# Tile 1's norm moved ahead of the first flag, with the checks of weights spread among the opening's work

## What is computed

```
xn  = layernorm(x)
out = x + attn(xn) + ffn(xn)
attn: x1 = xn + dwconv3(xn);  n = ln(x1)
      act = silu(n @ actp_w + b);  xi = silu(dwconv3(n @ in_w + b))
      q, k = elu(xi @ qk_w + b) + 1;  linear attention with rope over 16 heads, + dwconv3(v)
      x1 += (attention * act) @ out_w;  x1 += dwconv3(x1);  x1 += gelu(ln(x1) @ fc1) @ fc2
ffn:  h = silu(xn w1) * (xn w2);  h = gelu(h h1);  h = gelu(h h2);  out = h w3      (ternary weights)
```

## Time and profile before

| | us |
|---|---|
| median of 3 runs | 1124.96 |
| lowest, highest | 1118.63, 1132.96 |
| the profiled execution's own time | 1125.7 |
| its span in the trace | 1123.7 |
| mean granted clock of TensorE | 0.977 |

### The profile page before, as it was taken

The page is one execution under the profiler, slowest core; times in us unless marked ns, Lnnn a source line. Parts: engine busy times, 40 slices in busy tenths (PEclk is TensorE's granted clock), DMA queues, the critical chain, the costliest instruction groups (busy, mean ns, idle before and its releaser), DMA issues.

```text
span 1123.7 us, 17165 instructions
## 1 busy us (share of the span) xinstructions
PE 1044.5 (93%) x6636; PEld 922.7 (82%) x6636; DVE 767.7 (68%) x950; ACT 592.8 (53%) x853; POOL 282.2 (25%) x232
## 2 busy tenths in 40 slices
PE   3779988999999999899998999999989999999997
PEld 3557876888777677678877889899889899999997
DVE  6685567554546647988787538669677787776764
ACT  3356766666624345455544545465545456555543
POOL 3243334331514241442333003203300111011100
PEclk9899989999999999899999999999999999999999
DMA  8859963544585455212440084252486331332310
GB/s 333 323 188 310 346 206 113 187 160 161 172 328 197 136 183 206 93 55 97 169 150 38 37 327 160 77 169 76 134 301 260 113 110 50 104 113 76 113 38 20
DMA packets 68337, 180.67 MB, mean 161 GB/s; under 512 B 4976, under 2 KB 26096, under 8 KB 64624
## 3 DMA queue, kind: packets, MB, share of 16 engines
q1 hardware_dynamic: 68256, 179.56, 46.0%
HBM read 121.86 MB, written 66.06 MB: 167 GB/s over the span
## 4 chain that ended last, share of the span: by engine, by line
PE 68%; DVE 13%; ACT 6%; DMA 5%; issue 5%; POOL 2%; SPq 1%; DVEq 0%; ACTq 0%; POOLq 0%
PE pr L2078 42%; PE pr L192 12%; PE pr L2245 7%; DVE x L1465 3%; DVE h_lo L1702 2%; PE pr L178 2%; PE pr L185 2%; PE pr L2056 1%; DMA xn_s<-xh 1%; DMA qa<-q_s 1%; DVE acc L1495 1%; PE pr L2200 1%; DVE full L1567 1%; DMA h_s<-silu 1%; ACT h_hi L1280 1%
## 5 line engine op out<-in xcount | busy, mean ns | idle before, releaser
L2078 PE MATMUL pr<-xp_hi,wb 128*128 128x256 f32 x1344 | 323.1, 283 | 6.9 <-DVE u L1830 4.0
L2078 PE MATMUL pr<-xp_lo,wb 128*128 128x256 f32 x1344 | 322.5, 283 | 0.0
L2078 PEld LDWEIGHTS pr<-xp_hi,wb 128*128 128x128 f32 x1344 | 257.4, 192 | 9.0 <-issue 9.0
L2078 PEld LDWEIGHTS pr<-xp_lo,wb 128*128 128x128 f32 x1344 | 258.0, 192 | 0.0
L2078 PE MATMUL pr<-u_hi,ring 128*128 128x512 f32 x256 | 102.3, 399 | 2.3 <-issue 1.3
L2078 PE MATMUL pr<-u_lo,ring 128*128 128x512 f32 x256 | 100.0, 391 | 0.0
L1024 POOL TENSOR_TENSOR ot<-ot,yg 128x512 f32<-128x512 f32 x14 | 25.2, 1805 | 253.2 <-DVE ot L1861 253.2
L1340 ACT CAST xp_hi<-tf 128x1024 fp32r<-128x1024 f32 x48 | 50.2, 1047 | 65.1 <-PE pr L2078 24.2
L1702 DVE TENSOR_TENSOR h_lo<-hf,h_hi 128x512 fp32r<-128x512 f32 x64 | 59.8, 953 | 23.8 <-ACT h_hi L1280 23.8
L2245 PE MATMUL pr<-wf_hi,h_hi 128*128 128x256 f32 x256 | 75.0, 293 | 0.0
L1824 DVE TENSOR_TENSOR xp_lo<-tf,xp_hi 128x1024 fp32r<-128x1024 f32 x48 | 60.8, 1266 | 19.9 <-ACT xp_hi L1340 19.8
(11 more groups left out here) (224 smaller groups left out, 2583.2 us busy)
## 6 DMA issues: line engine op xcount, KB each, us to landing
ring<-w_s SPq DMA_DIRECT2D x42, 512.0 KB, 5.2
uf<-h_s SPq DMA_DIRECT2D x16, 1024.0 KB, 5.8
wb<-s_s SPq DMA_DIRECT2D x8, 1024.0 KB, 8.7
stage<-w_gated SPq DMA_DIRECT2D x4, 1536.0 KB, 10.4
wb<-w_s SPq DMA_DIRECT2D x6, 1024.0 KB, 10.0
vw<-v_s SPq DMA_DIRECT2D x8, 514.0 KB, 6.6
xt<-x SPq DMA_DIRECT2D x8, 512.0 KB, 6.5
xn_s<-xh SPq DMA_DIRECT2D x8, 512.0 KB, 8.1
```

The costliest lines, as they stand in the source:

```text
L2078: return e.matmul(bank, w.bitcast(dt), v_.bitcast(dt), start=first, stop=last, skip_group_check=True)
```

## The change

Everything concerns the opening and step -1.

- SyncE issues `save_xn(0)` after the second `stage` load and the load of tile 3, ahead of the third and fourth `stage` loads.
- Tile 1's `conv1_side`, `norm_tokens`, `norm_moments`, `inverse_deviation`, `norm_offsets`, `apply_norm`, `norm_back`, `high_of_norm` move from step -1 into the opening, before the first flag. `low_of_norm(1)` on VectorE comes right after the flag. In step -1 these are left out (`and i >= 0`).
- `norm_back(0)` goes ahead of `a_channels(2)` on TensorE, and `high_of_norm(0)` ahead of `copy_xn(2)` on ScalarE; `xi_out(0)` and `apply_norm(1)` go ahead of `high_of_xg(0)`.
- VectorE's twelve checks, before in groups of 3, 1, 2 and 6, are now in groups of 1, 1, 2, 4, 1 and 3.

The core of the diff (SyncE, POOL, ScalarE, VectorE, TensorE in this order):

```diff
                 if n < 2:
                     load_x(2 + n)
-            save_xn(0)
+                if n == 1:
+                    save_xn(0)
             load_xg(0, xg1)
...
             halo(2, xh, "xh_w", 1, "xh_halo")
+            inverse_deviation(1, "b", "b_applied")
             low_of_xg(0, xg1_lo, xg1, xg1_hi)
...
             apply_norm(0)
+            high_of_norm(0)
             copy_xn(2)
-            high_of_norm(0)
+            xi_out(0)
+            apply_norm(1)
             e.wait_ge(s["checked"], 3)
             e.wait_ge(s["w_in"][0], 16)
             e.wait_ge(s["w_in"][1], 16)
             high_of_xg(0, xg1_hi, xg1)
-            xi_out(0)
             act_out(0)
+            high_of_norm(1)
...
-            check_staged(range(0, 3))
+            check_staged(range(0, 1))
             conv1_side(0, False)
             conv1_side(0, True)
             xn_moments(2)
             norm_moments(0)
-            check_staged(range(3, 4))
+            check_staged(range(1, 2))
+            norm_offsets(0, "b", "b_applied")
+            low_of_attn_weights()
             apply_xn(2)
-            norm_offsets(0, "b", "b_applied")
-            check_staged(range(4, 6))
-            low_of_attn_weights()
+            check_staged(range(2, 4))
             low_of_norm(0)
-            check_staged(range(6, 12))
+            conv1_side(1, False)
+            conv1_side(1, True)
+            check_staged(range(4, 8))
+            norm_moments(1)
+            check_staged(range(8, 9))
+            norm_offsets(1, "b", "b_applied")
+            check_staged(range(9, 12))
             set_flag(0, front_bank[0][0:1, 0:1])
+            low_of_norm(1)
             for i in P1_STEPS:
...
                 norm_tokens(0)
+                norm_back(0)
                 a_channels(2)
-                norm_back(0)
                 in_proj(0)
                 act_proj(0)
+                norm_tokens(1)
+                norm_back(1)
...
-                    if valid(i + 2):
+                    if valid(i + 2) and i >= 0:
                         norm_tokens(i + 2)
...
-                    if valid(i + 2):
+                    if valid(i + 2) and i >= 0:
                         norm_back(i + 2)
```

More of the change, by code:

```diff
@@ L1197, in _ @@
                 front("p", i, "after_q")
-                if valid(i + 2) and i < 0:
-                    apply_norm(i + 2)
-                if valid(i + 2):
+                if valid(i + 2) and i >= 0:
                     high_of_norm(i + 2)
```

## The result

The changed kernel's median was 1115.61 us, that of the kernel before beside it 1126.32; the ratio is 0.9898, 95% interval 0.9857 to 0.9938. Run again in another job (12 executions against 27) it was 1116.21 against 1124.97: 0.9929, interval 0.9900 to 0.9957. By the medians the change gains 8.8 to 10.7 us, by the two ratios 0.7 to 1.0% (8 to 11 us). The forecast, 1120.5, said 4.4: the direction, the small size and the range were right, and half of the gain was not foreseen.

The account below looks back on a forecast made before the run. TensorE, busy 93% of the span, was taken as nearly the bound from 73.99 us on, the cheap time lying in the opening. First gate +5.0, step -1 -9.7 + 0.3 gave -4.4: 1124.96 to 1120.5 us, range 1113 to 1128.

Parts of the forecast that it names:

- (a): Step -1 without tile 1: 64 gate and up matmuls without stops, 16.65 us against 26.34, 9.7 less, 0.3 allowed back.
- (b): VectorE's list before the flag: gains 4.9 us, loses a 2.19 wait; in_proj(0) near 31.3, flag 49.8.
- the walk: VectorE's new list before the flag, timed item by item against the old: first gate at 51.0 if no check is disturbed.
- (c): Opening: GpSimd's low_of_xg(0) under VectorE's last checks costs 0 to 2.0 us, taken 1.6; first gate 52.6, 5.0 later.
- (d): Opening, SyncE's queue: save_xn(0) ahead of two stage loads lands near 23, worth nothing by itself; if it failed, copy_xn(2) 1.3 late.
- (e): The 3 MB copy into w_s behind the first gate lands at 66.7, not 61.74; ring refills keep over 10 us cover.
- The sum: First gate +5.0, step -1 -9.7 + 0.3: -4.4 us, step 0 at 69.6 instead of 73.99, median 1120.5.
- the first paragraph of the working: From 73.99 TensorE is nearly the bound; the opening's and step -1's savings are gained if later steps keep their length.
- Absorbed: Rival: transfers bound 98 to 160 us, so a 4.4 us earlier start gives nothing: 1124 to 1126; chance 0.17.
- Slower: Rival: tile 1's round trip delays the flag; gain gone at a first gate of 57.0, up to 1127.5; chance 0.08.
- More gain: Rival: GpSimd disturbs no check in the opening; first gate 49.9 to 51.0, saving 6 to 7, 1118 to 1119; chance 0.17.

Follow-up runs that it names:

- the two kept busy: Changed kernel with 28 extra TensorE matmuls ahead of the flag: 1113.2 us; changed kernel without the transfer's move, with 36 extra: 1111.9 us, 0.9880 of the kernel before.
- its two relatives: Kernel before with the transfer's move alone: 1124.7 us, ratio 1.0004; kernel before with 25 extra TensorE matmuls in its stops: 1122.7 us, ratio 0.9969.

## Why the prediction was right, and what it missed

**(a) Step -1** was 16.65 + 0.3 by the sum, and 17.17, 17.29 and 16.71 in three profiles. Right in total; its halves were each off, by luck to opposite sides. The first 32 matmuls took 9.9 us and not 9.15, since some twelve ran at the half clock where the rows of before have eight, and the other 32 took 7.25 and not 7.5. Tile 3's `apply_xn` took its longer time (3.30) and `a_channels(3)` waited 1.31 for it; that lies in step 0 in both kernels.

**(b) DVE's list** was right in its first half (`in_proj(0)` 31.3; it was 31.63). In the second the walk has nothing between check 8 and the offsets for POOL's inverse deviation, as if the check covered it. It didn't: the check stretched POOL's addition from 0.20 to 1.09, and DVE stood 1.18 us for it, at both tiles. That is one term I had at nothing. PE's transposes of tile 1, done at 40.44 and not at 40.9 to 42.0, and a gate 0.96 and not 1.14 behind the written flag (1.14 was PE's idle time) made up for most of it, so the walk's 51.0 was only 0.3 off.

**(c) The contention** was the term mis-sized: 1.6 taken, nothing measured at the place I had named. POOL's operation started at 47.75, when the last check (47.3) already ran, and then lay beside the maximum, which took its 1.22. The runs show the rule behind it, for two-input operations of VectorE and operations of POOL that both work from SBUF: who has started first keeps the other out for its whole length. POOL first cost a check 2.0 (before, and with the old groups), a spare operation 0.9, and the offsets 2.1; DVE first cost POOL's small addition 0.9, and `low_of_xg(0)` some 0.7 (3.03 behind a running check, 2.34 when it came first). The maximum, with one input in SBUF, lay beside `low_of_xg(0)` in seven profiles and took 1.22 in each. The Trainium skill (SBUF — State Buffer, Who interferes with whom) says just this, and the gate worked out by its rule, 51.0, was better than mine, 52.6; it was 51.3. That left the forecast's gate 1.3 us late.

**(d) The transfer's move** is worth nothing that the totals show in either kernel, as the sum had it (alone, within 3.5 us either way). Alone its positions were better than I allowed, by 0.6 to 2.4 us against the three profiles, and that did not reach the end.

**(e)** was right: the refill was issued at 65.11, and PE waited for no transfer from 60 to 125.

**The sum** said 4.4 us at `in_proj(1)`. In three profiles each the means are 73.4 and 68.0: 5.4. Here two terms missed to opposite sides: the gate was 3.0 us later and not 5.0, and step -1 was 8.4 shorter and not 9.4, since the kernel before took 25.1 and 24.9 us for it in its other two profiles and not 26.34. The larger part of the error, though, is in the first paragraph of the working: "if step 0 and those after it keep their length", with the length read from one execution. From `in_proj(1)` to `low_of_v(1)` the kernel before took 45.2, 49.5 and 49.4; the first profile, on which all stood, was the exception. The changed kernel took 45.6 in all three. So the lead grows by 2.4 on the average, to 7.8 us, of the 9 to 11 measured. In the two slower profiles of before the 3.9 us more than in the changed kernel are these: 1.0 is the longer stop before `a_channels(3)` (2.3 against 1.3), some 1.2 is half clock behind it, in 74 to 86, and 1.6 is half clock in 98 to 112 (0.86 and 0.88 of the clock there, 1.00 in all three profiles of the changed kernel).

What of this the change brings about is only partly shown. The first place lies behind a stop of 2.3 us before `a_channels(3)` that the change shortens to 1.3, and filling the stops removed the half clock behind it, not the stop. The second lies behind a stop of 2.48 us before `a_channels(4)`, which both kernels have: the changed one kept its clock there in three profiles, three relatives of it (with high_of_xg early, and the two kept busy) had 0.88, 0.92 and 0.90, and three others 1.00. Of the five profiles of the kernel before and its two relatives, four had the lower clock there. Why one comes through and another doesn't stays open. The last 1 to 3 us come later: in the means of three profiles the lead is 7.9 at 180 us, 8.6 at 211, 9.6 at 490 and 9.9 at the end of the spans. The first step is the one slow stretch of the first profile of before (33.4 against 31.2); what makes the others is open, and so is the total of the kernel with the old groups. No run has the new order of tile 0 alone (`norm_back(0)` ahead of `a_channels(2)`, with `in_proj(0)` 3.6 us earlier), so how much of the gain is its own is not shown.

**The rivals.** *Absorbed* is refuted: a gate 3.7 us later cost 3.5 at `low_of_v(1)`, 3.6 at `low_of_v(3)` (176 us) and about 5 at the end, and the changed kernel's own lead, 7.8 at `low_of_v(1)`, was 7.9 at `low_of_v(3)`. *Slower* had its break-even at a first gate of 57.0; with the old groups of checks the gate started at 56.38 and the gain was gone. *More gain* was right in its mechanism (no check disturbed) and still too small in its gain: 1118 to 1119 against 1115.6.

## What to carry to other kernels

Work moved ahead of a gate pays only if the round trips that it brings are filled with work that had to be done there anyway: twelve checks in another grouping made the difference between a gain and none. Before costing a change of half a per cent, profile the same kernel two or three times, and take the length of a stretch from all of them; one profile may be the lucky one. Where VectorE and GpSimd both work from SBUF, look at which of them starts first, by a tenth of a microsecond if need be, and put a reduction, not an operation of two inputs, beside a long one of GpSimd.

## What the runs showed that I had not expected

An operation of 0.16 us on VectorE took 2.29, because GpSimd had started a subtraction of 1024 columns 0.06 us earlier. And the granted clock fell 1.5 us after TensorE had resumed work, at 52.4, while it was busy: with 28 extra matmuls the gates began at the full 2.4 GHz, ran 1.5 us and then fell to 1.2 for eight matmuls. With the idle time around the flag itself filled as well it stayed up, in the one profile of that kernel.
